# Attention scores issued in groups of three pairs of matmuls, transposed rows copied by ScalarE and divided by GpSimd, and three smaller edits

## The reference

```python
xn = layernorm(x)
Q = (xn @ Wq.T).reshape(H, b, s, dkh)      # H = 16; K and V the same way
scores = einsum('hbqd,hbkd->hbqk', Q, K)
out = einsum('hbqk,hbkd->hbqd', softmax(scores), V).reshape(b, s, -1)
y = out + xn
attention = (y - mean(y, axis=(1, 2))) / sqrt(var(y, axis=(1, 2)) + EPS)
logits = xn @ w_gate.T                      # top 2 of 8, softmax of the two
experts = sum over e of gate[e] * (xn @ w_in[e].T) @ w_out[e].T
```

## Time and profile before

| | us |
|---|---|
| median of 3 runs | 1027.0 (1026.38 to 1034.03) |
| the profiled execution | 1026.8 |
| its span, first to last instruction | 1024.7 |
| PE busy | 1000.6 (98%) |
| DVE busy | 801.2 (78%) |
| ACT busy | 678.7 (66%) |
| POOL busy | 175.2 (17%) |

### The profile page before, as it was taken

The page is one execution under the profiler, slowest core; times in us unless marked ns, Lnnn a source line. Parts: engine busy times, 40 slices in busy tenths (PEclk is TensorE's granted clock), DMA queues, the critical chain, the costliest instruction groups (busy, mean ns, idle before and its releaser), DMA issues.

```text
span 1024.7 us, 20748 instructions
## 1 busy us (share of the span) xinstructions
PE 1000.6 (98%) x7816; PEld 521.8 (51%) x7816; DVE 801.2 (78%) x1023; ACT 678.7 (66%) x1355; POOL 175.2 (17%) x325
## 2 busy tenths in 40 slices
PE   6999999999999999999999999999999999999995
PEld 6888888888766333333333333333333333333332
DVE  4343464533555799999999999999999999999976
ACT  2313333433322688888888888888888888888885
POOL 2002444444454100000000000100000000000000
PEclk9999999999999799999999999999999999999998
DMA  9967432222300133433333333333333333332204
GB/s 348 370 239 224 130 132 81 74 77 82 107 1 2 47 95 84 94 89 93 90 91 92 85 97 87 92 91 92 92 84 96 88 95 88 91 92 73 67 21 166
DMA packets 127043, 108.59 MB, mean 106 GB/s; under 512 B 81120, under 2 KB 102368, under 8 KB 126944
## 3 DMA queue, kind: packets, MB, share of 16 engines
q1 hardware_dynamic: 122720, 102.81, 34.8%
q10 hardware_dynamic: 4224, 4.46, 1.2%
HBM read 80.75 MB, written 42.21 MB: 120 GB/s over the span
## 4 chain that ended last, share of the span: by engine, by line
PE 96%; DVE 1%; POOL 1%; issue 1%; DMA 1%; ACT 0%; SPq 0%; POOLq 0%; DVEq 0%
PE ps L1004 28%; PE ps L986 23%; PE ps L942 17%; PE ps L974 11%; PE ps L899 6%; PE ps L871 4%; PE ps L887 2%; PE ps L1015 2%; PE ps L1027 1%; PE ps L860 1%; DMA wp<-w_out_t 1%; DVE stage L835 0%; DVE xn L830 0%; DVE stage L849 0%; POOL wp L381 0%
## 5 line engine op out<-in xcount | busy, mean ns | idle before, releaser
L696 DVE TENSOR_REDUCE negm<-ps 128x1 f32<-128x1024 f32 x512 | 618.6, 1223 | 33.5 <-PE ps L974 14.6
L541 ACT ACTIVATE wp<-ps 128x512 f32<-128x512 f32 x680 | 367.3, 603 | 51.1 <-PE ps L986 22.6
L986 PE MATMUL ps<-qf,kf 50*128 50x512 f32 x1024 | 389.1, 457 | 1.2 <-ACT wp L490 1.2
L974 PE MATMUL ps<-kf,qf 48*128 48x512 f32 x1024 | 369.5, 450 | 0.0
L986 PEld LDWEIGHTS ps<-qf,kf 50*128 50x128 f32 x1024 | 160.5, 186 | 206.6 <-ACT wp L541 108.9
L1004 PE MATMUL ps<-wp,vb 128*17 128x256 f32 x2720 | 213.9, 387 | 0.2 <-issue 0.2
L974 PEld LDWEIGHTS ps<-kf,qf 48*128 48x128 f32 x1024 | 146.9, 186 | 6.3 <-issue 5.9
L541 ACT ACTIVATE picks<-ps 128x512 f32<-128x512 f32 x172 | 103.6, 603 | 26.1 <-PE ps L986 12.9
L490 ACT ACTIVATE wp<-ps,gates 128x256 f32<-128x256 f32 x128 | 53.7, 471 | 93.8 <-PE ps L942 93.8
L687 DVE SCALAR_TENSOR_TENSOR acc<-ps,gates,acc 128x256 f32<-128x256 f32 x64 | 30.8, 482 | 103.1 <-PE ps L942 103.1
L1004 PEld LDWEIGHTS ps<-wp,vb 128*17 128x17 f32 x2720 | 46.8, 96 | 118.4 <-ACT wp L541 44.0
(11 more groups left out here) (110 smaller groups left out, 834.1 us busy)
## 6 DMA issues: line engine op xcount, KB each, us to landing
qk_d<-stage SPq DMA_DIRECT2D x64, 256.0 KB
feat_d<-qk_d SPq DMA_DIRECT2D x64, 256.0 KB, 3.3
qf<-feat_d SPq DMA_DIRECT2D x128, 128.0 KB
qf<-feat_d SPq DMA_DIRECT2D x128, 64.0 KB
kf<-feat_d SPq DMA_DIRECT2D x128, 64.0 KB
v_d<-vstage ACTq DMA_DIRECT2D x8, 544.0 KB, 5.0
vb<-v_d SPq DMA_DIRECT2D x128, 34.0 KB, 2.4
acc<-x SPq DMA_DIRECT2D x8, 512.0 KB, 6.8
```

Of the source, the lines that this page charges most:

```text
L541: nc.scalar.activation(weight_tile(n, j, b)[:, h * HALF:(h + 1) * HALF], ps[:, ST_BANK[(2 * unit + b) % 3], :], ACT.Exp).then_inc(exp_done, 1)
L696: nc.vector.tensor_reduce(negm[:, n % 2, qt:qt + 1], ps[:, b:b + 2, :].rearrange("p b c -> p (b c)"), AX.X, ALU.max, negate=True).then_inc ...
L974: last = nc.tensor.matmul(ps[:, MAX_BANK[turn % 2] + half, :], qf[rows, u, qt * P:(qt + 1) * P], kf[rows, u, :], start=True, stop=True)
L986: nc.tensor.matmul(ps[:, ST_BANK[(2 * unit + half) % 3], :], kf[rows, u, j * P:(j + 1) * P], qf[rows, u, h * HALF:(h + 1) * HALF], start=T ...
```

## The change

Five things change.

1. **Order of loads.** The first expert weights are asked for ahead of the first tokens.
2. **End of the expert stage.** In the last eight token tiles the two `max_scores` of a tile stand together after `y_bank(t, 1)`, where each stood behind its own bank; VectorE's `maxima` follow. `Y_BANK` becomes (4, 5, 7, 6), and the wait of TensorE for all four banks ahead of the first head is replaced by a wait of each of the first three score tiles for its own bank and of the first sum for bank 6. `max_halves(1)` on GpSimd moves ahead of the last tile's sums.
3. **Groups of three.** Pairs of matmuls are issued one by one, and after every third (one and a half units) as many sums follow as are due: one and two in turn.
4. **The copy of a head's sums** (`pv_out`) moves from behind the seventh exponent of the next head to behind its ninth.
5. **Transposed rows.** ScalarE copies them from PSUM (`copy_rows`), GpSimd raises the denominators to the power -1, multiplies, and adds to `xn`. Only for the last pair VectorE still takes the reciprocal. `served` turns a turn's number into the count of `turn_done`, since the row turns no longer count there.

```diff
-        Y_BANK = (4, 5, 6, 7)
+        Y_BANK = (4, 5, 7, 6)
...
+            load_weights(0, 0)
             load_x(0)
-            load_weights(0, 0)
...
             def residual(pair):
-                pool.wait_ge(turn_done, row_turn[pair] + 1)
-                nc.gpsimd.tensor_tensor(xn[:, bass.ds(pair, 1), :].rearrange("p o d -> p (o d)"),
-                                        xn[:, bass.ds(pair, 1), :].rearrange("p o d -> p (o d)"),
-                                        att[:], ALU.add).then_inc(y_done, 1)
+                pool.wait_ge(rows_copied, pair + 1)
+                if pair < NB // 2 - 1:
+                    nc.gpsimd.tensor_tensor(rden[:], rows[:, :, :, DH], minus[:], ALU.pow).then_inc(rows_step, 1)
+                pool.wait_ge(rows_step, 2 * pair + 1)
+                nc.gpsimd.tensor_tensor(rows[:, :, :, 0:DH], rows[:, :, :, 0:DH],
+                                        rden[:].unsqueeze(3).to_broadcast([P, 4, 4, DH]), ALU.mult).then_inc(rows_step, 1)
+                pool.wait_ge(rows_step, 2 * pair + 2)
+                tile = xn[:, bass.ds(pair, 1), :].rearrange("p o (c g d) -> p (o g) c d", c=4, g=4)
+                nc.gpsimd.tensor_tensor(tile, tile, rows[:, :, :, 0:DH], ALU.add).then_inc(y_done, 1)
...
+            def copy_rows(pair):
+                turn = row_turn[pair]
+                act.wait_ge(turn_ready, turn + 1)
+                if pair:
+                    act.wait_ge(y_done, pair)
+                nc.scalar.copy(rows[:], ps[:, MAX_BANK[turn % 2], :].rearrange("p (g c v) -> p g c v", g=4, c=4)[:, :, :, 0:VW]
+                               ).then_inc(rows_copied, 1)
+
             for n in range(NB):
                 for j in range(NKT // 2):
                     for h, b in ((0, 0), (0, 1), (1, 0), (1, 1)):
                         exps(n, j, h, b)
-                        if (j, h, b) == (LAG - 1, 1, 0) and n:
+                        if (j, h, b) == (LAG, 0, 0) and n:
                             pv_out(n - 1)
+                    if j == LAG and n % 2 == 0 and n:
+                        copy_rows(n // 2 - 1)
...
             def free_turn(turn):
                 if turn >= 2:
-                    pe.wait_ge(turn_done, turn - 1)
+                    if turn - 2 in row_turns:
+                        pe.wait_ge(rows_copied, row_turns.index(turn - 2) + 1)
+                    else:
+                        pe.wait_ge(turn_done, served(turn - 2))
...
-            def crossed_scores(n, j, h):
-                scores(n, j, h, 0)
+            def crossed_scores(n, j, h, half):
+                scores(n, j, h, half)
                 if n + 2 < NB:
-                    max_scores(n + 2, 2 * j + h, (1,))
-                    max_scores(n + 2, 2 * j + h, (0,))
-                scores(n, j, h, 1)
+                    max_scores(n + 2, 2 * j + h, (1 - half,))
...
+            def sum_until(unit):
+
+                while summed[0] < unit - 2 * LAG:
+                    n, tile = divmod(summed[0], NKT)
+                    sum_values(n, tile // 2, tile % 2)
+                    summed[0] += 1
+                    if tile == NKT - 1:
+                        if n + 2 < NB:
+                            maxima_to_rows(n + 2)
+                        break
 
             for n in range(NB):
                 for j in range(NKT // 2):
                     for h in range(2):
-                        crossed_scores(n, j, h)
+                        for half in range(2):
+                            crossed_scores(n, j, h, half)
+                            tiles = 2 * (NKT * n + 2 * j + h) + half + 1
+                            if tiles % len(ST_BANK) == 0:
+                                sum_until(tiles // 2)
```

More of the change, by code:

```diff
@@ L126, in attention_and_experts @@
         rden = sb("rden", [P, 4, 4])
-        att = sb("att", [P, D])
+        rows = sb("rows", [P, 4, 4, VW])
+        minus = sb("minus", [P, 4, 4])
         ystat = sb("ystat", [P, NT, 6])
@@ L224, in attention_and_experts, with served @@
         row_turn[NB // 2 - 1] = next_turn()
+        row_turns = list(row_turn.values())
+        def served(turn):
+            return turn + 1 - sum(row <= turn for row in row_turns)
         def feature_loads(n):
@@ L357, in _ @@
             nc.gpsimd.memset(onesm[:], 1.0 / P).then_inc(const_step, 1)
-            for value, tile in ((-0.5, mhalf), (EPS, epst), (0.0, zero)):
+            for value, tile in ((-0.5, mhalf), (EPS, epst), (0.0, zero), (-1.0, minus)):
                 nc.gpsimd.memset(tile[:], value).then_inc(const_step, 1)
@@ L703, in first_rows @@
                                       ).then_inc(turn_done, 1)
[L705 to L715, removed]
             def statistics(pair):
@@ L743, in _ @@
                 qk_lo_half(1, o)
[L744 removed]
+            dve.wait_ge(const_step, 7 + E)
             first_choice(0)
@@ L762, in _ @@
                             qk_lo_half(c, 2 * (i - 2) + j)
-                    if t >= NT - 2 * TC:
-                        n, qt = divmod(2 * (t - NT + 2 * TC) + j, NKT)
+                for i_max in range(2 * (t - NT + 2 * TC), 2 * (t - NT + 2 * TC) + 2):
+                    if i_max >= 0:
+                        n, qt = divmod(i_max, NKT)
                         maxima(n, qt)
@@ L1044, in _ @@
                     y_bank(t, j)
[L1045 to L1055 removed]
+                    if j == BY_VECTOR - 1:
+                        for i in range(2 * (t - NT + 2 * TC), 2 * (t - NT + 2 * TC) + 2):
+                            n, qt = divmod(i, NKT)
+                            max_scores(n, qt)
+                            if n == 1 and qt == 1:
+                                maxima_to_rows(0)
+            summed = [0]
+            def sum_until(unit):
[7 more added lines that the diff above has]
+                        break
             for n in range(NB):
@@ L1066, in _ @@
                             mean_over_partitions(0, slice(0, EARLY), j // 2)
-                        if j >= LAG:
-                            sum_values(n, j - LAG, h)
-                        elif n:
-                            sum_values(n - 1, NKT // 2 + j - LAG, h)
-                        if n and j == LAG - 1 and h == 1 and n + 1 < NB:
-                            maxima_to_rows(n + 1)
-            for j in range(NKT // 2 - LAG, NKT // 2):
-                for b in range(2):
-                    sum_values(NB - 1, j, b)
+            for n in range(2):
+                sum_until(NKT * NB + 2 * LAG)
             to_token_rows(NB // 2 - 1)
```

42 lines of the change are left out of this document (19 added, 23 removed).

## The result

| | before | after |
|---|---|---|
| median, us | 1027.0 | 1086.8 (1084.4 to 1088.2, 4 runs) |
| profiled execution | 1026.8 | 1088.2 |
| its span | 1024.7 | 1086.4 |
| two heads, mean of 27 | 21.08 | 23.04 |
| first score of the second head | 347.1 | 345.5 |

After is slower: the ratio is 1.057, 95% interval 1.053 to 1.061, or +60 us. The prediction said 1067, with 1086 as its upper end. The last four lines of the table come from the starts of score tiles in the two timelines, and say where the time is: 60.5 us in the heads and 2.9 in the tail (from the last score to the end), less 1.6 at the start.

What follows compares the result with a forecast made beforehand. TensorE looked full in the heads, VectorE following with 0.1 us to spare a unit. From 1026.8: heads +43, tail +1, loads -1, maxima together -3, heads' start -1, last two heads +1, giving 1067 us, range 1028 to 1086.

Steps and rivals of the forecast that it cites:

- the loop from U2's tiles through VectorE back to the third pair: In the heads, tiles waiting for maxima's banks make three units take 3.94 us, 1.31 a unit against 1.23 now.
- U2: The middle of three units, split: one tile is the last pair of a group, the other the next group's first.
- two conditions for failure: A maximum releasing its banks well before its record ends, or the third pair's wait letting the queue behind go on.
- late pair: A group's last pair, loaded late after waiting for its banks; it holds TensorE 0.44 us until the next shape's load.
- The sums for TensorE alone: Groups without waits: 0.90 us a group, 0.55 one sum, 0.98 two; 3.33 us for three units, 1.11 a unit.
- heads' ends: Transposes, row turns and exponent-delaying copies on top of the loop: 1.5 us per two heads, bounds 0.3 and 2.2.
- the exponents' loop: In the heads, a group's third exponent frees the bank for the next group's third tile: 3.58 us for three units.
- The rows: Transposed rows on ScalarE and GpSimd: power 2.8 us for 16 elements, covered in the heads; tail +1.0 us (0.7 to 1.8).
- The small edits: Order of loads -1 us, maxima together in the last eight token tiles -3, the start of the heads -1.
- Clock: Granted clock averages 0.58 from 333 to 349 us, behind gaps; staying at 1.00 would save some 6 us more.
- TensorE alone: Rival, chance 0.06: TensorE alone decides in the heads, 0.12 us saved in each of 490 units, 967 us.
- The second rival: Exponents decide, not maxima, in the heads: 3.58 us for three units, 1.19 each, 1006 us; chance 0.07.

Runs made afterwards that it cites:

- Run 2: The kernel before with only the groups of three and the later copy of a head's sums; 1087.2 us, ratio 1.060.
- run 5: The changed kernel with each maximum cut into two reductions, each freeing its own bank, plus a small minimum a head; 1034.6 us, ratio 1.010.
- run 6: The changed kernel with two sums in place of one between a split unit's two tiles, same instructions; 1141.2 us, ratio 1.112.
- run 8: The kernel before with the small edits, groups of three and maxima cut in halves, rows divided on VectorE; 1023.2 us, ratio 0.996.
- Run 11: The changed kernel with VectorE's 30 `statistics` moved behind the last maximum; one execution, 1091.1 us, two heads 22.81 us.
- run 7: The changed kernel with GpSimd's power for the means put ahead of the last but one residual; 1087.1 us, tail 20.2 us.
- run 3: The kernel before with only the transposed rows moved to ScalarE and GpSimd, no groups; 1031.8 us, ratio 1.006.
- Run 9: The changed kernel with run 7's move and that pair's `statistics` on VectorE behind its scaling pieces; 1083.3 us, ratio 1.054, tail 16.6 us.
- run 1: The kernel before with only the order of loads and both edits at the end of the expert stage; 1021.2 us, ratio 0.996.
- run 4: The changed kernel with each maximum reading one of its two banks and the exponent scaled down, output not the attention; 1024.5 us, ratio 0.999.
- run 10: The kernel before with small edits and rows on ScalarE and GpSimd, no groups, tail queues reordered, last multiplication on VectorE; 1024.2 us, ratio 0.997.

## Why the prediction was right, and where it was off

**Direction and mechanism: right.** The prediction's main step, the loop from U2's tiles through VectorE back to the third pair, is there link by link (3.94 us predicted, 3.96 found), and so are its marks: maxima in threes with one longer gap (1.69 for 1.7), 129 waits for VectorE, less busy time on TensorE, a chain through VectorE. Run 2 places it in the groups, run 5 shows that it isn't VectorE's amount of work, and run 6 that its period follows one link. Of its two conditions for failure, neither came: the banks are freed at the record's end (447.28 + 1.22 = 448.50, and the load at 448.55), and the sum's load comes 0.43 us behind the late pair.

The sums for TensorE alone stand too: in run 8 a group takes 0.91 us from its first load to the sum's (490.27 to 491.18, 0.90 predicted), and the two sums 0.99 (0.98). The Trainium skill's rule that a change of the tiling mode drains TensorE (TensorEngine Tiling (Array Packing), Key Properties) agrees with this; no run varied the changes of mode alone. What fewer of them save is taken away again by one loop or the other.

**Size: 20 us too small in all, 17 of them in the heads, which took the result 0.8 us over the upper end.** In two heads 23.04 us were found and 22.5 predicted. 16 units at 1.32 are 21.1 of it, 0.1 more than I had, so +4 us over 30.4 such pairs. The two places of low clock are 2 us. The term that was mis-sized is "heads' ends", 1.5 us taken and 1.8 found (22.96 less 21.12), +10 us. I took today's value, which is 1.4 and not 1.5 (16 x 1.23 is 19.7), and argued that the loop would hide a part. No hidden part shows in the sum. What stands at a head's end goes, at least in part, into the loop's own links. The turn of the rows shows it:

```profile
642.40 0.42 PEld L1033 LDWEIGHTS ps<-ident,ot 128*128 128x128 f32 x4 [0.90 <-ACT ot L566]
...
643.47 0.18 PEld L989 LDWEIGHTS ps<-kf,qf 48*128 48x128 f32 x1 [0.30 <-DVE negm L720]
...
643.89 0.56 PEld L1022 LDWEIGHTS ps<-wp,vb 128*17 128x17 f32 x16 [0.24 <-issue]
...
645.45 3.48 DVE L720 TENSOR_REDUCE negm<-ps 128x1 f32<-128x1024 f32 x3 [2.04 <-PE ps L989]
```

Transposes, a late pair and two sums follow each other, and VectorE stands for 2.04 us. Run 11 puts 0.15 us of the 1.8 down to `statistics`. Of the 5.5 us that six heads of run 7 take over 10.56 each, 4.3 are in the three heads with a turn of the rows (2.4, 1.4 and 0.5), so the same turn costs more or less by where in a group it falls. How this divides between the transposes, the turn and the group that a head's eight units cut short was not measured apart; in run 8, where the exponents' loop sets the pace, the same remainder (21.08 less 16 x 1.19) is 2.0 us, in run 6, with slower cycles, 1.4.

**The rows: right in the heads, off in the tail.** No cost in the heads (run 3: 21.04), as predicted; GpSimd's power took 2.91 us where 2.8 was worked out. The tail was +2.9 where I had +1.0, the second term that was mis-sized. I had followed the power to `statistics` and the halves of the maxima, but not to the power for the means, `brstd`, which stands behind it in GpSimd's queue just once, at the end. Run 9 takes 2.1 us of it out again, which leaves 0.8.

**The small edits: right in sum, wrong in the parts.** Predicted -5, and run 1 gives -4.5; in the profiled execution of after only 1.6 of it shows, since a low clock took 1.5 us in the expert stage (below). The token tiles went as worked out, 6.82 to 6.44 us in the chain:

```profile
280.14 5.78 PE ps L954 x24
285.92 0.66 PE ps L989 x4
286.58 5.78 PE ps L954 x24
```

so 0.38 us less in each of eight. The order of loads was worth nothing. The first matmul starts 1.9 us earlier than in the earlier trace rows, and then waits for 2.17 us:

```profile
6.26 5.62 PEld L911 LDWEIGHTS ps<-wp 128*128 128x128 f32 x16 [6.26 <-DMA wp<-w_out_t]
...
14.06 2.02 PEld L911 LDWEIGHTS ps<-wp 128*128 128x128 f32 x10 [2.17 <-DMA wp<-w_out_t]
```

The first token tile's matmuls begin at 87.0 us, 86.5 in run 1, 86.0 before; over the ten traces with the new order it is 85.3 to 87.1, over the three with the old one 86.0 to 86.3. I had priced the first wait and not looked at the next.

**Clock.** I forecast that it would stay low behind the heads' start, and it did: 0.57 for 0.58. What I hadn't foreseen are further dips, one in the expert stage and two in the heads, below; they cost the profiled execution of after 3.5 us.

**The rivals.** TensorE alone (967; 0.12 us in 490 units are 59 us and not 57, so 965) never came up: neither run 4 (21.07 us for 16 units, 1.32) nor run 8 (1.19 in a cycle) comes near 1.11 us a unit. The second rival's price (3.58 us) was exact; its time, 1006, was too low by the same heads' ends as my own, with 1.5 us where the groups make 2.0. So the groups could not have gained here even with VectorE out of the way: 16 x 1.19 + 2.0 is 21.1, what the kernel before takes.

## What to carry to other kernels

When an order is regrouped, do not ask which engine is full but follow each buffer around: from the matmul that fills it, through the engine that reads it, to the next matmul that needs it, and add up what stands in the queues between. The longest such loop divided by the units in it was the floor here, and an engine that was busy for 83% of the stretch held it. A long instruction that frees two buffers at once is a long link; two short ones that free one each gave back 52 of 60 us here for the same work. And when an operation gets slower on an engine with plenty of time, look through its whole queue, the tail included, and then through the queue of the engine that waits for it: run 7 failed because the same 2.9 us stood in both.

## What the runs showed of the hardware

**Two reductions of one bank cost little more than one of two.** The record of a maximum of 512 elements is 679 ns, of 1024 elements 1218 ns; on end they start 0.60 and 1.14 us apart. Cutting it in two costs VectorE 0.06 us.

**The same waits were followed by a lower clock in some executions and not in others.** With the maxima together in the expert stage, TensorE waits for GpSimd's halves of the first head; in the profiled execution of after this was followed by 3.4 us in which loads came 0.43 us apart in place of 0.23:

```profile
307.73 0.09 PEld L1043 LDWEIGHTS ps<-ident,mpart 128*16 128x16 f32 x1 [2.28 <-POOL mpart L420]
...
309.05 0.33 PEld L954 LDWEIGHTS ps<-mtl,xth 128*128 128x128 f32 x1
309.48 0.33 PEld L954 LDWEIGHTS ps<-mth,xtl 128*128 128x128 f32 x1
...
311.50 0.19 PEld L954 LDWEIGHTS ps<-mtl,xth 128*128 128x128 f32 x1
311.73 0.19 PEld L954 LDWEIGHTS ps<-mth,xtl 128*128 128x128 f32 x1
```

The granted clock of 303 to 312 us is 0.81 there (the stretch shown at the top), so a part of it at the lower of the two levels, 1.2 GHz. All ten kernels with this edit have the wait, and TensorE is busy for 7.14 to 7.16 of those 9 us in each. In after and runs 4, 5, 6, 9 and 11 the clock is 0.81 over them; in runs 1, 7, 8 and 10 it stayed at 1.00. Where it fell, this token tile took 9.6 to 9.9 us from its first matmul to the next tile's, against 8.4.

The same happened in the heads. After (first two lines) and run 7, 1.48 us earlier in its span (last two), at the same turn of the rows, with the same columns as at the top:

```profile
564.10:574.10 10.00, 9.12 (x75) 4.11 (x78) 8.34 (x8) 7.84 (x16) 0.85 (x3) 1.00 0.37 92
574.10:577.60 3.50, 3.50 (x26) 1.39 (x27) 1.02 (x1) 1.65 (x4) 3.34 (x3) 0.51 0.43 95
...
562.62:572.62 10.00, 9.14 (x75) 4.10 (x78) 8.33 (x8) 7.84 (x16) 0.84 (x3) 1.00 0.36 92
572.62:576.12 3.50, 3.50 (x43) 1.70 (x40) 2.05 (x2) 2.37 (x5) 3.34 (x3) 1.00 0.46 97
```

What TensorE did in the ten us before is the same to 0.02 us, and only one of the two fell to the lower level; those two heads took 24.89 us in after and 23.90 in run 7. Before and runs 1, 3 and 10, with units of two pairs, have no such place between 349 and 990 us; run 2 has two, run 4 one, run 6 four and run 9 two. The Trainium skill (TensorE: Matmul & The Clock Gate, Part 1: The HAM clock gate) has these two levels and ties the lower one to an idle TensorE; what decides between two executions that idle alike no run here shows.

**GpSimd's power goes by its elements**: 2.91 us for 16, 0.86 for three, 0.56 for one, where a multiplication of 256 elements takes it 0.62.
